# A of tile 0 loaded in rows and transposed on TensorE, x of tile 1 in two transfers, and a new order of the last tile

## The reference, cut to what matters

```python
W = weights[condition]                                   # (64, 32, 32)
x = x + jnp.einsum('bct,bcd->bdt', x, W)
base_out = jnp.einsum('bti,oi->bto', x, W1) + b          # W1: 512 x 512
A, Bm = lora_As[adapter_mapping], lora_Bs[adapter_mapping]   # (64, 512, 16), (64, 16, 512)
lora_h = jnp.einsum('bti,bir->btr', x, A)
x = x + base_out + jnp.einsum('btr,bro->bto', lora_h, Bm) * 2.0
```

## Time and profile before

| | us |
|---|---|
| median of 3 runs | 85.22 (85.2 to 85.53) |
| the profiled execution, its own time | 85.35 |
| its span, first to last instruction | 83.6 |
| PE busy | 79.6 (95% of the span) |
| DVE, ACT and POOL busy | 59.3, 52.0 and 35.0 |
| read from memory, written | 11.74 MB, 4.19 MB |

### The profile page before, as it was taken

The page is one execution under the profiler, slowest core; times in us unless marked ns, Lnnn a source line. Parts: engine busy times, 40 slices in busy tenths (PEclk is TensorE's granted clock), DMA queues, the critical chain, the costliest instruction groups (busy, mean ns, idle before and its releaser), DMA issues.

```text
span 83.6 us, 1999 instructions
## 1 busy us (share of the span) xinstructions
PE 79.6 (95%) x521; PEld 71.8 (86%) x521; DVE 59.3 (71%) x154; ACT 52.0 (62%) x179; POOL 35.0 (42%) x75
## 2 busy tenths in 40 slices
PE   4999999999999999999999999999999999999970
PEld 2368688999899999999999999999999999999930
DVE  2048495885888787777878787888787777876540
ACT  1545757766566675958666666666685957669120
POOL 6128888844442617080715344342617080303000
PEclk9999999999999999999999999999999999999999
DMA  0999779899776768676586878676874734120333
GB/s 13 307 347 315 143 199 261 165 365 329 209 239 163 239 196 245 197 206 213 143 250 171 238 178 241 174 248 151 219 211 159 177 110 152 45 92 7 119 125 125
DMA packets 15997, 16.06 MB, mean 192 GB/s; under 512 B 10225, under 2 KB 10482, under 8 KB 15986
## 3 DMA queue, kind: packets, MB, share of 16 engines
q1 hardware_dynamic: 14016, 11.74, 47.4%
q0 software_dynamic: 1248, 4.06, 17.0%
q10 hardware_dynamic: 722, 0.14, 0.9%
HBM read 11.74 MB, written 4.19 MB: 191 GB/s over the span
## 4 chain that ended last, share of the span: by engine, by line
PE 85%; DMA 6%; ACTq 3%; ACT 2%; issue 1%; DVE 1%
PE z_ps L548 58%; PE z_ps L585 9%; DMA a_raw<-in_lora_a 6%; PE y_ps L596 4%; PE y_ps L600 4%; PE y_ps L598 4%; PE ht_ps L572 2%; ACTq L323 1%; PE z_ps L580 1%; PE ht_ps L626 1%; ACT L317 1%; PE y_last L608 1%; PE y_ps L608 1%; ACTq L313 1%; DVE y_sb L534 1%
## 5 line engine op out<-in xcount | busy, mean ns | idle before, releaser
L548 PE MATMUL z_ps<-wa,x_hi 128*128 128x288 f32 (+2 forms) x240 | 50.3, 301 | 0.0
L548 PEld LDWEIGHTS z_ps<-wa,x_hi 128*128 128x128 f32 x240 | 38.0, 188 | 1.8 <-issue 0.5
L548 PE MATMUL z_ps<-wa,x_lo 128*128 128x288 f32 (+2 forms) x120 | 35.5, 296 | 0.0
L548 PEld LDWEIGHTS z_ps<-wa,x_lo 128*128 128x128 f32 x120 | 22.6, 188 | 0.0
L291 POOL DMA_INDIRECT b_raw<-in_lora_b,b_index_slot x16 | 17.6, 1097 | 4.4 <-POOL b_index_slot L289 4.4
L300 POOL CAST m_hi<-m_raw 128x128 fp32r<-128x128 f32 x15 | 4.4, 293 | 31.5 <-ACT m_raw L337 31.5
L480 DVE TENSOR_TENSOR z_lo<-z_ps,z_hi 128x256 fp32r<-128x256 f32 x30 | 11.3, 420 | 6.4 <-ACT z_hi L381 6.4
L381 ACT CAST z_hi<-z_ps 128x256 fp32r<-128x256 f32 x30 | 9.7, 376 | 9.7 <-PE z_ps L585 9.6
L337 ACT COPY m_raw<-w_raw 32x32 f32 x64 | 13.8, 216 | 1.8 <-DVE w_raw L502 1.2
L439 DVE TENSOR_TENSOR x_lo<-x_raw,x_hi 128x512 fp32r<-128x512 f32 x14 | 9.7, 690 | 3.5 <-ACT x_hi L349 3.5
L460 DVE TENSOR_TENSOR b_lo<-b_raw,b_hi 128x512 fp32r<-128x512 f32 x15 | 10.4, 693 | 1.6 <-ACT b_hi L369 1.1
(11 more groups left out here) (51 smaller groups left out, 78.8 us busy)
## 6 DMA issues: line engine op xcount, KB each, us to landing
out<-y_sb SPq DMA_DIRECT2D x15, 256.0 KB, 2.4
x_raw<-in_xt SPq DMA_DIRECT2D x14, 256.0 KB, 2.9
a_raw<-in_lora_a SPq DMA_DIRECT2D x60, 32.0 KB
first_sb<-in_first SPq DMA_DIRECT2D x2, 384.0 KB, 4.0
first_sb<-in_first SPq DMA_DIRECT2D x3, 256.0 KB, 4.8
b_raw<-in_lora_b,b_index_slot POOLq DMA_INDIRECT x16, 4.0
bias_sb<-in_bias SPq DMA_DIRECT2D x1, 256.0 KB, 5.2
out<-y_sb SPq DMA_DIRECT2D x2, 128.0 KB, 1.7
```

What stands on the lines that cost most here:

```text
L548: done = nc.tensor.matmul(target, (x_lo if lo_x else x_hi)[s][:, k, :], moving(lo_w), start=first and not lo_x and not lo_w, stop=last and ...
```

## The change

It has three parts.

First, A of tile 0. The host lays out a second copy of the A matrices with t in rows (`lora_a_rows`, 16 x 512 for each adapter). ACT's four transfers bring 16 rows of 2 KB each into `a0_rows` (64 partitions). PE transposes its four chunks into PSUM between `first_chunk(1)` and `first_chunk(2)`, and ACT copies the result to `a0_sb`. SP no longer waits for `a0_ready` before it loads A of tile 3.

Second, the order around tile 1. x of tile 1 becomes two pieces of `first`, of half the size; SP issues the second behind A of tile 1. ACT and DVE take tile 1's A between its two halves of x. The index of the gathers moves from POOL to DVE (`index_b`), behind two additions of the identity.

Third, the end. The transpose and adapter product of tile 14 come earlier on PE, the second half of tile 15's chunks 2 and 3 comes behind its first adapter product. The last mix is done in a split half (`mix_last_half`, three float32r passes) and two float32 quarters (`mix_last_quarter`), with three bias additions and three stores, the last of them issued by ACT. POOL splits the last tile's matrix, too.

```diff
-    PIECES = (0, X0_AT[1], W_AT[2], W_AT[3], X1_AT, X1_AT + T)
-    PIECE_OF_X1 = 4
+    PIECES = (0, X0_AT[1], W_AT[2], W_AT[3], X1_AT, X1_AT + T // 2, X1_AT + T)
+    PIECE_OF_X1 = (4, 5)
+    PARTS = (slice(0, HALF), slice(HALF, HALF + P), slice(HALF + P, O))
...
+        def a0_in_psum(k):
+            return y_last[:, 0:KC * JR].rearrange("p (k q) -> p k q", k=KC)[:, k, :]
+        def y_part(n):
+            return (y_ps[LAST % 2][:, 0:HALF], y_last[:, 0:P], ht_ps[:, 0:P])[n]
...
# SP
             def load_a(u):
-                if u == NA:
-                    sp.wait_ge(a0_ready, 1)
-                elif u > NA:
+                if u > NA:
                     sp.wait_ge(a_ready, 2 * (u - NA))
...
-            for n in range(len(PIECES) - 1):
+            for n in range(PIECE_OF_X1[0] + 1):
                 load_first(n)
             sp.wait_ge(ids_loaded, 16)
             load_a(1)
+            load_first(PIECE_OF_X1[1])
             load_x(2)
...
-            for half in range(2):
-                sp.wait_ge(y_ready, LAST + 1 + half)
-                sp.dma_start(out_rows[LAST * P:(LAST + 1) * P, cols(half)],
-                             y_sb[LAST % 2][:, cols(half)]).then_inc(y_stored[LAST % 2], 16)
+            for n, at in enumerate(PARTS[:-1]):
+                sp.wait_ge(y_ready, LAST + 1 + n)
+                sp.dma_start(out_rows[LAST * P:(LAST + 1) * P, at],
+                             y_sb[LAST % 2][:, at]).then_inc(y_stored[LAST % 2], 16)
...
# POOL
-            pool.wait_ge(ids_p_loaded, 16)
-            pool.tensor_copy(r_of_p[:, :], ids_p_sb[:, TILES:TILES + 1]).then_inc(r_ready, 1)
-            pool.wait_ge(r_ready, 1)
-            pool.tensor_scalar(b_index[:, :], ids_p_sb[:, 0:TILES], float(R), r_of_p[:, 0:1],
-                               ALU.mult, ALU.add).then_inc(b_index_ready, 1)
             pool.wait_ge(b_index_ready, 1)
...
-            for u in range(LAST):
+            for u in range(TILES):
                 split_m(u)
...
# ACT
             for j in range(J):
                 slot = act.snap(adapters0[j], min_val=0, max_val=SLOTS - 1)
-                act.dma_start(a_raw[0][:, j:j + 1, :, :].rearrange("p j k r -> p j (k r)"),
-                              lora_a[bass.ds(slot, 1)].rearrange("s p k r -> p s (k r)")
-                              ).then_inc(a_loaded[0], 16)
+                act.dma_start(a0_rows[j * R:(j + 1) * R, :],
+                              lora_a_rows[bass.ds(slot, 1)].rearrange("s r t -> (s r) t")).then_inc(a0_loaded, 16)
...
             round_w(2)
+            act.wait_ge(a0_transposed, 1)
+            act.copy(a0_sb[:, :, :], a0_in_psum(slice(0, KC))).then_inc(a0_ready, 1)
             round_x1(0)
-            act.wait_ge(a_loaded[0], 16 * J)
-            act.copy(a0_sb[:, :, :].rearrange("p k (j r) -> p k j r", j=J),
-                     a_raw[0][:, :, :, :].rearrange("p j k r -> p k j r")).then_inc(a0_ready, 1)
+            round_a(1)
             round_x1(1)
-            round_a(1)
             round_w(KC - 1)
...
             build_m(LAST - 1)
-            build_m(LAST)
-            round_h(LAST)
             for half in range(2):
                 round_z(LAST - 1, half)
-            for half in range(2):
-                act.wait_ge(lora_done, 2 * LAST + half + 1)
-                act.copy(z_sb[:, cols(half)], z_of(LAST, half)).then_inc(z_copied, 1)
+            round_h(LAST)
+            build_m(LAST)
+            round_z(LAST, 0)
+            act.wait_ge(lora_done, 2 * LAST + 2)
+            for n in range(2):
+                act.copy(z_sb[:, n * P:(n + 1) * P], z_of(LAST, 1)[:, n * P:(n + 1) * P]).then_inc(z_copied, 1)
+            act.wait_ge(y_ready, LAST + len(PARTS))
+            act.dma_start(out_rows[LAST * P:(LAST + 1) * P, PARTS[-1]],
+                          y_sb[LAST % 2][:, PARTS[-1]]).then_inc(last_part_stored, 16)
...
# DVE
+            def index_b():
+                dve.wait_ge(ids_p_loaded, 16)
+                nc.vector.tensor_copy(r_of_p[:, :], ids_p_sb[:, TILES:TILES + 1]).then_inc(r_ready, 1)
+                dve.wait_ge(r_ready, 1)
+                nc.vector.tensor_scalar(b_index[:, :], ids_p_sb[:, 0:TILES], float(R), r_of_p[:, 0:1],
+                                        ALU.mult, ALU.add).then_inc(b_index_ready, 1)
             add_identity(0)
-            for k in range(KC - 1):
+            add_identity(1)
+            index_b()
+            rest_w(0)
+            for k in range(1, KC - 1):
                 add_identity(k + 1)
                 rest_w(k)
             rest_x1(0)
+            rest_a(1)
             rest_x1(1)
-            rest_a(1)
             rest_w(3)
...
             rest_h(LAST - 1)
+            mask_ht(LAST - 1)
             rest_b(LAST)
-            mask_ht(LAST - 1)
             finish_y(LAST - 2)
-            rest_h(LAST)
             rest_z(LAST - 1, 0)
             rest_z(LAST - 1, 1)
+            rest_h(LAST)
             mask_ht(LAST)
             finish_y(LAST - 1)
+            rest_z(LAST, 0)
             dve.wait_ge(y_stored[LAST % 2], 16 * (LAST // 2))
-            for half in range(2):
-                dve.wait_ge(y_computed, LAST + 1 + half)
-                nc.vector.tensor_tensor(y_sb[LAST % 2][:, cols(half)], (y_ps[LAST % 2], y_last)[half][:, cols(half)],
-                                        bias_sb[:, cols(half)], ALU.add).then_inc(y_ready, 1)
+            for n, at in enumerate(PARTS):
+                dve.wait_ge(y_computed, LAST + 1 + n)
+                nc.vector.tensor_tensor(y_sb[LAST % 2][:, at], y_part(n), bias_sb[:, at], ALU.add).then_inc(y_ready, 1)
...
# PE
+            first_chunk(0)
+            first_chunk(1)
+            pe.wait_ge(ident_ready, 1)
+            pe.wait_ge(a0_loaded, 16 * J)
             for k in range(KC):
-                first_chunk(k)
+                last = nc.tensor.transpose(a0_in_psum(k), a0_rows[:, k * P:(k + 1) * P], ident[0:JR, 0:JR])
+            last.then_inc(a0_transposed, 1)
+            first_chunk(2)
+            first_chunk(3)
             pe.wait_ge(a0_ready, 1)
...
             last_chunk(1, 0)
+            transpose_h(LAST - 1)
             mix(LAST - 2)
-            transpose_h(LAST - 1)
+            lora(LAST - 1, 0)
+            lora(LAST - 1, 1)
             last_chunk(2, 0)
             last_chunk(3, 0).then_inc(main_done, 1)
-            lora(LAST - 1, 0)
-            lora(LAST - 1, 1)
             last_chunk(0, 1)
             last_chunk(1, 1)
             transpose_h(LAST)
-            last_chunk(2, 1)
             mix(LAST - 1)
             lora(LAST, 0)
+            last_chunk(2, 1)
             last_chunk(3, 1)
             lora(LAST, 1)
-            mix_last(0)
-            mix_last(1)
+            mix_last_half()
+            mix_last_quarter(0)
+            mix_last_quarter(1)
```

More of the change, by code:

```diff
@@ L14, with lora_residual_program @@
 ALPHA = 32
-def lora_residual_program(nc, first, xt, ids_row, ids_of_p, w0, bias, lora_a, lora_b, out):
+def lora_residual_program(nc, first, xt, ids_row, ids_of_p, w0, bias, lora_a, lora_a_rows, lora_b, out):
     _, _, KC, _ = xt.shape
@@ L84, in lora_residual_program @@
         a_raw = [sb(f"a_raw{s}", [P, J, KC, R], F32) for s in range(NA)]
+        a0_rows = sb("a0_rows", [JR, T], F32)
         a0_sb = sb("a0_sb", [P, KC, JR], F32)
@@ L98, in lora_residual_program @@
         z_lo = [sb(f"z_lo{s}", [P, O], F32R) for s in range(2)]
-        z_sb = sb("z_sb", [P, O], F32)
+        z_sb = sb("z_sb", [P, HALF], F32)
         y_sb = [sb(f"y_sb{s}", [P, O], F32) for s in range(2)]
@@ L113, in lora_residual_program @@
         a_loaded = [sem(f"a_loaded{s}") for s in range(NA)]
+        a0_loaded = sem("a0_loaded")
         a1_half_loaded = [sem(f"a1_half_loaded{half}") for half in range(2)]
@@ L116, in lora_residual_program @@
         y_stored = [sem(f"y_stored{s}") for s in range(2)]
+        last_part_stored = sem("last_part_stored")
         zeros_ready = sem("zeros_ready")
@@ L136, in lora_residual_program @@
         a_ready = sem("a_ready")
+        a0_transposed = sem("a0_transposed")
         a0_ready = sem("a0_ready")
@@ L250, in _ @@
             store_y(LAST - 1)
-            for half in range(2):
-                sp.wait_ge(y_ready, LAST + 1 + half)
-                sp.dma_start(out_rows[LAST * P:(LAST + 1) * P, cols(half)],
-                             y_sb[LAST % 2][:, cols(half)]).then_inc(y_stored[LAST % 2], 16)
+            for n, at in enumerate(PARTS[:-1]):
+                sp.wait_ge(y_ready, LAST + 1 + n)
+                sp.dma_start(out_rows[LAST * P:(LAST + 1) * P, at],
+                             y_sb[LAST % 2][:, at]).then_inc(y_stored[LAST % 2], 16)
             sp.wait_ge(y_stored[0], 16 * (TILES // 2))
             sp.wait_ge(y_stored[1], 16 * (TILES // 2 + 1))
+            sp.wait_ge(last_part_stored, 16)
         @block.gpsimd
@@ L340, in round_x1 @@
             def round_x1(half):
-                if half == 0:
```

(27 more changed lines are left out.)

## The result

The changed kernel takes 86.23 us, median of 4 runs (86.12 to 86.53); the kernel before took 85.37 beside it (85.2 to 85.53). The ratio is 1.0106 [1.0075, 1.0137]: 0.9 us slower, where 84.7 was forecast. The profiled execution took 86.19, its span 84.5. Times here are medians of all executions of a kernel, while the ratios leave out those that took over 1.5% longer than its fastest or ran at a lower granted clock.

A forecast was written before the change was run, and what follows sets the result against it. The prediction took TensorE, busy in 95% of the span, as the bound. From 85.35 us profiled, head -0.15, clock -0.10 and end -0.35 gave 84.75, so 84.7 for the median; range 84.0 to 85.4.

The forecast's parts named there:

- I take 7.1: Head: tile 0's A was put landing at 7.1 us, 0.4 before PE asks, within 6.0 to 9.12.
- A still lands late: Rival, head: A lands at 9.12 again with chunks 2 and 3 behind the wait; 86.4 us, chance 0.08.
- the later holes: Tile 1's A, the first gather and tile 3: three waits to close, -0.40 us together.
- the wait for A: Head: PE's hole of 0.35 us before tile 0's products with A and 0.05 of slow restart go, -0.40.
- Transposes and both changes of shape: Head, PE: four transposes come in at +0.45 us and two changes of array shape at +0.20.
- The 0.16 that I read as leaving the shape: First adapter product: 1.02 us instead of 0.86 was read as the cost of leaving the 64-row shape, entering hidden.
- The wait for tile 1's A: Tile 1's first product on PE no longer waits for A's split on DVE: -0.10 us, ends -0.20 and 0.
- The wait for the first gather: PE's hole before the first adapter product goes, the gather going out about 1.3 us earlier: -0.15 us.
- The hole in tile 3: Tile 3's four adapter passes, 0.64 us against 0.50 in tile 2, lose their hole: -0.15 us.
- The clock: Head: PE's step from 1.2 to 2.4 GHz at about 6.87 us may come earlier or later; booked at -0.10.
- The end: Last microseconds, tile 15's split mix and bias sums: -0.35 us, within -0.15 and -0.55.
- the 1.6 among its signs: Sign of being right: 1.6 us instead of 1.96 from the last adapter pass to the last bias sum.

The follow-up runs named there:

- e2: The changed kernel, but A of tile 0 loaded and reordered as before, without transposes: 85.33 us, ratio 0.997 to the kernel before.
- e10: e2 with the gathers' index on POOL again: 84.71 us, ratio 0.9943 to the kernel before.
- e14: e2 with the second and third gather held until A of tile 2 has landed: 88.31 us, ratio 1.0263 to the kernel before.
- e16: e10 with four useless transposes of 64 rows added in each of tiles 4, 7, 10 and 13: 86.66 us, ratio 1.0192 to the kernel before.
- e1: The kernel before with the new end alone: 84.93 us, ratio 0.996 to the kernel before.
- e4: The changed kernel with the transposes behind the third chunk instead of the second: 85.57 us, ratio 1.0021 to the kernel before.
- e5: The changed kernel without its new end: 86.45 us, ratio 1.0153 to the kernel before.
- e7: The changed kernel with the gathers' index on POOL again: 86.46 us, ratio 1.0151 to the kernel before.
- e15: The changed kernel with the transposes behind the third chunk and the gathers' index on POOL: 85.39 us, ratio 1.0026 to the kernel before.
- e9: The changed kernel, but SP loads tile 0's A from fixed adapters in one transfer between pieces two and three: 86.45 us, ratio 1.0143 to the kernel before.
- e12: e6 with the gathers' index on POOL: 86.77 us, ratio 1.0166 to the kernel before.
- e13: e9 with the gathers' index on POOL: 85.75 us, ratio 1.0046 to the kernel before.
- e8: The changed kernel, but SP issues nothing behind the fifth piece until A of tile 0 has landed: 91.82 us in one execution.
- e3: The changed kernel, but ACT loads tile 0's A early from fixed adapters, without waiting for the adapter numbers: 85.96 us, ratio 1.0108 to the kernel before.
- e6: The changed kernel, but SP issues two of tile 0's four A transfers ahead of the third piece, ACT two: 86.52 us, ratio 1.0157 to the kernel before.

## Why the prediction was wrong

**The step that failed** is "I take 7.1". It stood between 6.0 and 9.12, and the true value was 8.52. I argued from the quickest landing on empty DMA engines and from A's place beside the fourth and fifth piece; but A landed behind the fifth piece (7.87), as it had before the change (9.12 behind 8.15). That order was in the trace of before, and it was the better estimate. With it the wait of 1.14 us, which the forecast had at nothing, came with 1.73 us of products behind it. The larger pieces of A gained nothing: in kernels with x of tile 1 in halves and A in ACT's queue, A landed at 8.46 to 8.64 in the old form (e2, e10, e14, e16) and at 8.35 to 8.56 in rows; with the whole x it was 9.12, and 9.31 in e1. What the rows did was to delay the fifth piece, from 7.34 to 7.47 in the old form to 7.66 to 7.87 (the changed kernel, e4, e5, e7, e15). What A gained came with the halving of the fifth piece, the one thing in which the head's transfers of e1 and e10 differ.

**The rival was right, its chance was not.** "A still lands late" named the place, the two chunks behind the wait, and the point from which it decides, 8.1. Its working, with the products with A 0.6 earlier for a landing at 8.52, gives 85.22 + 1.3 - 0.4 - 0.35 = 85.8. The 0.4 up to 86.23 are 0.15 in the median of before (85.37 beside this run), 0.05 at the products with A, 0.1 in the later holes (-0.30 in the table), 0.07 in the end, and 0.07 behind the last sum. I gave it 0.08, as if A had only a small chance beyond 8.1, where the bounds I had set (6.0 to 9.12) left a third of their length there.

**The other terms of the head**, with the wait for A taken out (1.35 - 1.14 = +0.21 at the products with A, forecast -0.40 + 0.45 + 0.20 = +0.25):

- Transposes and both changes of shape: forecast 0.65, measured 0.47 here, where the wait hides the step in, and 0.5 to 0.57 in e16. The three steps between transposes are 0.06 to 0.09 each, not 0.11. The 0.16 that I read as leaving the shape was both changes: before, the first of the four passes took 0.29 instead of 0.216 and the last 0.30, and the first pass behind them 0.24 instead of 0.13. The products with A now pay 0.09 for the change into their own shape, which the wait for A hid before.
- The wait for tile 1's A (-0.10): nothing. In both kernels the first passes behind the products with A are 0.20 and 0.24 apart, with the data there: the loss is a change of shape, the end of the range that I named and did not take.
- The wait for the first gather (-0.15): -0.12, of which the adapter product's slower first pass takes 0.03 back. The gather went out 1.46 earlier and the hole before the adapter product is gone but for the change of shape. (DVE's smallest operations were put at 0.2 from the earlier trace rows, which show none under 0.285; the two took 0.15 and 0.23.)
- The hole in tile 3 (-0.15): 0.64 became 0.49 in the chain, but the term was right by luck. In e1, with the old head, these passes take 0.48, and in e16, whose third gather goes out at 12.08 and not at 11.80 as before, 0.48 too. The third gather landed 7.6 after its issue in the profiled execution of before, but 4.9 after it in e1 and 5.3 in e16; the slow landing, and the hole with it, most likely belonged to that one execution. Tiles 1 to 14 together gained 0.21, this included.
- The clock (-0.10): the step fell at 6.94 in this execution, 6.85 before, so nothing. Over the profiled executions it fell anywhere from 4.0 to 7.1.

**The end** (-0.35) was right: -0.28 from the last adapter pass to the end of the last bias sum, what e1 gives alone, and up to 0.06 more ahead of it, within the -0.21 of the middle. The distance is 1.68, the forecast's own 81.05 - 79.37 (the 1.6 among its signs was rounded too far). The way there is another, though: the forecast had DVE wait for the quarters, but the first bias sum starts 0.74 after the last adapter pass and the three follow each other without a gap, 0.93. DVE is the bound there, not ACT's copies.

**What the forecast did not have at all** is A of tile 2. I priced the earlier gather by who waits for it, and one more transfer ahead of x of tile 2 at nothing; I didn't ask what the gathers would collide with. They hold A of tile 2 up by 1.1 to 1.4 us. It cost the changed kernel nothing, but PE stood for it in the profiled executions of e2 (1.17 us) and e9 (1.81 us), and it is the likely reason why e2 stopped at 85.33 and e9 lost what it had gained.

**What stays open.** e12 and e9 show A of tile 2 late also when SP issues it later, and e14 that gathers hold it up; how much of e9's 14.14 is the one and how much the other was not separated (e13, with the index on POOL, has 12.10 from the same issue). The second gather is the suspect: in the changed kernel, e2, e4, e5 and e9 it went out 0.5 to 0.7 us ahead of A's last transfer, and A of tile 2 landed 0.03 to 0.19 behind it; in e7, e10, e15 and e16 it went out behind and landed over 1.5 us later than A. But in e13 it went out 0.5 us ahead and A landed first all the same. The clock's step up fell at 4.0 to 7.1 in executions with nearly the same head, and no run tells what fixes it.

## What to carry to other kernels

A wait moved ahead on an in-order engine must be priced with the work that used to fill it: here 1.73 us of products stood before the wait and then behind it, so the landing time of one transfer decided the sign. Take a landing under load from the order of the landings around it, not from the quickest one, and give the wait a chance in proportion to its bounds. Look for a hole in a second kernel with the same head before its closing is booked as a gain; one profiled execution can have it to itself. And when a transfer is made to start earlier, look for the one that shares the DMA engines with it and who is queued behind that one.

## What the runs showed of the hardware that I had not expected

- A change of the array's shape between two products costs 0.09 to 0.2 us even when all data is there: the step into the four transposes, out of them (0.15, and a first pass of 0.32 instead of 0.216), from 64 columns back to 128 (0.20 and 0.24 instead of 0.11 and 0.13).
- Behind some waits of PE the clock fell, behind most it did not. In e7 PE stood 2.1 us ahead of the transposes, and the passes behind them took 0.216 each; the clock also stayed at 1.00 behind 1.81 us of idle time in e9 and 2.15 in e12. But in e14 it was 0.50 from 19.16 to 22.58, behind waits of 0.45 and 1.85 us before 16.18 and 18.96, and in e8 from 15.80 to 22.63, behind 1.55, 1.38 and 0.88 us before 8.56, 13.30 and 15.22. The Trainium skill ("TensorE: Matmul & The Clock Gate", Part 4: PE-mode transpose) says that transposes do not count as busy; no run here shows a cost of it.
- Issuing a transfer 1.1 us earlier moved its landing by 0.17 at most (e3); putting it ahead of three large ones moved it by 1.7 (e6) and, all of it in one queue, by 2.1 (e9).
- The gather's index takes 0.15 and 0.23 us on DVE (L502, L504), 0.91 on POOL for the second alone.
